# A tuned graph network kernel: POOL runs three waited-for fills behind every fourth row gather

## What is computed

```python
# first part: attention over the edges, and two hops of mean aggregation
msg = alpha[:, :, None] * h[src]
out = jax.ops.segment_sum(msg, dst, num_segments=N)
...
for _ in range(num_hops):
    h = jax.ops.segment_sum(h[src], dst, num_segments=N) / deg
# second part: five layers
for l in range(W1.shape[0]):
    h = _leaky(x @ W1[l] + b1[l]) @ W2[l] + b2[l]
    e = _leaky(edge_attr @ We1[l] + be1[l]) @ We2[l] + be2[l]
    msg = h[src] * e * dot_scale[l]
    agg = jax.ops.segment_sum(msg, dst, num_segments=n)
    out = x + agg * res_w[l]
    ...layer norm...
```

## Time and profile before

| what | us |
|---|---|
| median of 3 runs | 8059.58 |
| lowest and highest run | 8028.11, 8065.32 |
| span of the profiled execution | 8041.5 |
| PE busy | 5609.6 |
| DVE busy | 4833.5 |
| POOL busy | 4208.7 |
| ACT busy | 3995.4 |

### The profile page before, as it was taken

One profiled execution on the slowest core, in us unless ns is written; L12 is line 12 of the kernel. 1 busy time (PEld: TensorE's weight loads), 2 busy tenths in 40 slices (PEclk: granted clock), 3 DMA queues, 4 the chain that ended last, 5 costly groups with the idle time before them and its releaser, 6 DMA issues.

```text
span 8041.5 us, 131647 instructions
## 1 busy us (share of the span) xinstructions
PE 5609.6 (70%) x48820; PEld 4901.3 (61%) x48820; DVE 4833.5 (60%) x12225; ACT 3995.4 (50%) x6886; POOL 4208.7 (52%) x4251
## 2 busy tenths in 40 slices
PE   6787772333333788876788877888867888688886
PEld 5676651222222677776777766777757777577776
DVE  5565565566575566655666665566656666566666
ACT  3454444555564355553555544555535555355554
POOL 4454457666665355554555544555545555455554
PEclk8898775655555788887888887888878888689887
DMA  3333325767675233332233322323323333233322
GB/s 85 83 96 83 84 72 174 233 233 240 233 259 198 52 79 80 83 79 57 80 84 79 82 71 67 79 80 84 81 57 80 84 83 79 56 79 83 83 80 68
DMA packets 509356, 828.41 MB, mean 103 GB/s; under 512 B 112942, under 2 KB 220069, under 8 KB 495662
## 3 DMA queue, kind: packets, MB, share of 16 engines
q1 hardware_dynamic: 373374, 650.98, 24.0%
q0 software_dynamic: 135344, 169.01, 11.5%
HBM read 385.16 MB, written 434.48 MB: 102 GB/s over the span
## 4 chain that ended last, share of the span: by engine, by line
PE 36%; issue 12%; DVE 12%; another core or an unknown queue 7%; POOL 1%; ACT 1%; DMA 0%; DVEq 0%; SPq 0%; POOLq 0%; ACTq 0%
PE psum L1354 30%; DVE arena L1756 5%; PE psum L1368 5%; DVE by_lane L1819 2%; DVE psum L1802 1%; DVE es_w L1756 1%; POOL agg L700 1%; DVE gring L1796 0%; DVE psum L1808 0%; PE psum L1280 0%; PE psum L1311 0%; DVE xin L1756 0%; DVE gring L1756 0%; DMA agg<-rowsg,last_i 0%
## 5 line engine op out<-in xcount | busy, mean ns | idle before, releaser
L693 POOL DMA_INDIRECT gring<-tableh,src_i x2652 | 2600.3, 980 | 2529.9 <-DVE psum L1802 1560.1
L1354 PE MATMUL psum<-penalty,arena 125*128 125x192 bf16 x24736 | 2659.8, 260 | 611.6 <-issue 579.9
L1354 PEld LDWEIGHTS psum<-penalty,arena 125*128 125x128 bf16 x24736 | 2232.7, 103 | 859.3 <-issue 789.4
L693 POOL DMA_INDIRECT gring<-table,src_i x1364 | 1388.7, 1018 | 1031.9 <-issue 402.7
L1756 DVE TENSOR_SCALAR arena<-dst_f,node_id 125x640 bf16<-125x640 f16 x4556 | 1605.1, 401 | 0.1
L1796 DVE TENSOR_REDUCE gring<-psum 128x128 f32<-128x384 f32 x505 | 355.9, 705 | 1996.9 <-remote 1286.4
L967 ACT COPY psum<-diag 128x512 f32<-128x512 f32 x505 | 297.5, 590 | 2355.9 <-DVE psum L1802 2202.9
L1368 PE MATMUL psum<-arena 128*128 128x128 f32 x4040 | 706.3, 311 | 180.1 <-issue 164.8
L1368 PEld LDWEIGHTS psum<-arena 128*128 128x128 f32 x4040 | 601.2, 218 | 243.7 <-issue 241.8
L1486 DVE SCALAR_TENSOR_TENSOR arena<-psum,be_c,arena 128x512 f32<-128x512 f32 x505 | 376.7, 746 | 450.5 <-ACT arena L839 260.1
L839 ACT ACTIVATE arena<-psum,be_leak 128x512 f32<-128x512 f32 x505 | 335.9, 686 | 602.3 <-remote 410.6
(11 more groups left out here) (271 smaller groups left out, 7681.2 us busy)
## 6 DMA issues: line engine op xcount, KB each, us to landing
rows<-arena SPq DMA_DIRECT2D x101, 1296.0 KB
acts<-arena SPq DMA_DIRECT2D x505, 256.0 KB
arena<-acts SPq DMA_DIRECT2D x505, 256.0 KB
rowsg<-run SPq DMA_DIRECT2D x505, 256.0 KB
gring<-tableh,src_i POOLq DMA_INDIRECT x2652
dst_f<-pe_src SPq DMA_DIRECT2D x430, 93.8 KB
rows<-run SPq DMA_DIRECT2D x101, 256.0 KB
gring<-table,src_i POOLq DMA_INDIRECT x1364
```

Of the source, the lines that this page charges most:

```text
L693: pool.indirect_dma_start(ring[:, s, k, :], None, table, bass.IndirectOffsetOnAxis(ap=src_i[:, c * K + k:c * K + k + 1], axis=0))\
L1354: ins = mm(found(n)[:, m, :], hot_at(n // 2, j)[:, at:at + P], parts[:, j, :, :].rearrange("q a f -> q (a f)"), start=(j == 0), stop=(j == ...
```

## The change

POOL gets a helper, `pause`, that fills a scratch tile of 128 x 256 fp32 three times and waits for each fill before it goes on. `gather_chunk`, which all seven passes use, counts its gathers in one counter and calls `pause` before the fifth, the ninth and so on: behind every fourth gather, wherever the chunk borders lie. The gathers of node rows at the ends of the passes are not counted. To have a semaphore for it, `node_id_set` goes; the one instruction that raised it raises `consts_set` instead, whose full count goes up by one.

```diff
+BURST = 4
+REST = 3
...
+        rest = sb("rest", [P, 256])
...
+        rested = sem("rested")
...
             pool.iota(node_id[:, :], [[1, NJ]], base=-MID, channel_multiplier=NJ,
-                      allow_small_or_imprecise_dtypes=True).then_inc(node_id_set, 1)
+                      allow_small_or_imprecise_dtypes=True).then_inc(consts_set, 1)
...
+            issued, rests = [0], [0]
+
+            def pause():
+
+                for _ in range(REST):
+                    pool.memset(rest[:, :], 0.0).then_inc(rested, 1)
+                    rests[0] += 1
+                    pool.wait_ge(rested, rests[0])
+
             def gather_chunk(c, s, table, ring, ready, cols):
                 for k in range(cols):
+                    if issued[0] and issued[0] % BURST == 0:
+                        pause()
+                    issued[0] += 1
                     pool.indirect_dma_start(ring[:, s, k, :], None, table,
...
-            act.wait_ge(node_id_set, 1)
...
-            dve.wait_ge(node_id_set, 1)
...
-            dve.wait_ge(node_id_set, 1)
...
-N_CONSTS = 20
+N_CONSTS = 21
```

More of the change, by code:

```diff
@@ L339, in build @@
         src_in = [sem(f"src_in{b}") for b in range(2)]
-        found_ps, hot_done, parts_ready, node_id_set = (sem(n) for n in (
-            "found_ps", "hot_done", "parts_ready", "node_id_set"))
+        found_ps, hot_done, parts_ready = (sem(n) for n in ("found_ps", "hot_done", "parts_ready"))
         cg_ready, cg_used = sem("cg_ready"), sem("cg_used")
         early_set = sem("early_set")
+        rested = sem("rested")
         be_set = sem("be_set")
```

## The result

| what | before | after |
|---|---|---|
| median, us | 8062.45 (4 runs) | 6963.74 (4 runs) |
| lowest and highest, us | 8028.11, 8078.08 | 6958.54, 6970.45 |
| span of the profiled execution, us | 8041.5 | 6958.6 |

A forecast was written before the change was run, and what follows sets the result against it. The prediction took PE, kept slow in stretches by back-to-back gathers, as the bound: 8041.5 - 252 (layers) - 40 (layer starts) - 50 (hop) + 140 (attention) = 7840, plus 18 from span to median, said as 7860 us; range 7620 to 8260.

The forecast's parts named there:

- the price of a pause: On POOL, behind every fourth gather: three fills and their waits add 1.7 us to the gap, ends 1.4 and 2.0.
- the work of a pause on the slow stretches: On PE in the layers: pauses cut each slow stretch from 7.3 to 4 to 4.5 us.
- One sign of being wrong: In the layers: DVE waiting for gathers would mean POOL is the bound by more than reckoned; no size given.
- What bounds the kernel: Whole kernel: PE, kept slow by back-to-back gathers in 213 stretches, 1561 us; a gap of about 1.9 us ends one.
- The layers: Five layers: a chunk falls from 9.70 to 9.2 us, gaining 252 us, ends 379 us and nothing.
- Layer starts: At each layer's start: a pause breaks the stretch of 21 us, gaining 8 us a layer, 40 us (0 to 75).
- The hop pass: Hop pass: the same stretches, rarer; POOL needs 9.3 us a chunk against 10.8 now; gain 50 us (0 to 120).
- The attention pass: Attention pass: no countable slow stretches, POOL becomes the bound at 1434 us; 140 us longer (78 to 199).
- (a): Whole kernel: runs of four gathers never start a slow stretch, POOL is the bound everywhere; 7626 us, chance 0.15.
- (b): Whole kernel: pauses do not let PE out, stretches last until the run ends; 8680 us, chance 0.13.
- (c): Whole kernel: pauses work, but POOL's waits behind chunk ends and lost ring lead cost the gain; 8020 to 8100, chance 0.10.
- (d): Whole kernel: DVE stretches the pauses to 2.3 us, no gain in layers, attention + 240; about 8250 us, chance 0.10.

The follow-up runs named there:

- e7_before_again: The kernel before, unchanged, run again on a chip where it met hardly any slow stretches: 5724.71 us.
- e8_after_again: The changed kernel, unchanged, run again on a chip where the kernel before took 5724.6 us: 6910.39 us, ratio 1.208 to the kernel before.
- e6_one_fill: Against the changed kernel, one long fill of 1248 one-byte elements replaces the three in each pause: 6920.69 us, 1.209 of the kernel before on that chip.

## Why the prediction was wrong in its size

The steps that failed are two terms of the sum: the price of a pause, put at 1.7 us and measured at 1.15, and the work of a pause on the slow stretches, put at "4 to 4.5 us instead of 7.3" so that PE stays beside POOL as a bound, where no long stretch was left beside the paused gathers and POOL alone is the bound. Of the 896 us by which the measurement lies below the forecast, the layers make 502, the hop pass 172, the attention pass 157, layer starts 28, start-up and the rest 22, and the difference between span and median most of what is left. One sign of being wrong that the prediction named came: DVE waits for gathers in the layers, 395.3 us at L1815.

**What bounds the kernel.** Right where it was read: PE, held back in slow stretches beside long runs of gathers. But "I take it that gathers issued back to back keep PE slow" is too wide. e7_before_again has runs of 530 gathers and no such PE, so the earlier trace rows show a coincidence in time that holds on some chips only. This did not make the number wrong, since the kernel before took 8078.08 us in the one further run that the result has of it; it limits what the change is worth.

**One pause.** Forecast 1.7 us (1.4 to 2.0), measured 1.15 us, below the range's end. The working took three fills of 0.312 us and three waits of 0.24 us. But the 0.24 us of idle time stood before another operation, a select at L665 that waited for a fill, and not between two fills. In the row at 3807.64 three fills and the waits between them last 1.07 us, 0.94 us of it fills at 0.312, which leaves 0.06 us for each of two waits; over the whole trace all 2006 waits between two fills of a pause are 0.057 or 0.058 us. The last wait and the issue of the next gather cost 0.27 us together, in place of the ordinary 0.30, and not on top of it.

**The layers.** Forecast 9.2 us a chunk and 252 us gained; measured 8.25 to 8.32 and 754 us. The two mis-sized terms are the pause (1.31 times 0.55 us too much on POOL's side, 0.72 us a chunk) and the stretches, taken as shortened to 4 to 4.5 us, when none of four gaps was left in the steady part. With both put right POOL's need is 6.67 + 1.31 x 1.15 = 8.18 us a chunk, and that is what is measured within 0.14. The 0.25 us added for two sides waiting for each other was hardly there, at most 0.14: PE, at 744.41 us busy in a stretch of 880 us, has slack:

```profile
3340.00:4220.00 880.00, 744.41 (x7866) 713.09 (x7865) 679.51 (x1607) 535.07 (x719) 679.96 (x949) 0.93 0.35 92
```

The granted clock rose from 0.86 to 0.93, as the prediction's last part asked for. It is 0.91 in the same stretch of e8_after_again, where there are no slow stretches, and 1.00 in e7_before_again. So what it lacks goes with the idle time that the pauses bring: PE and DVE wait for gathers in both.

**Layer starts.** Forecast 40 us (0 to 75), measured 68 us for the tails and starts together: inside the range. The tails were not in the forecast, and they are only in part cured, as shown above: the gathers there are not paused.

**The hop pass.** Forecast 50 us (0 to 120), measured 222 us, 10.81 to 8.58 us a chunk. The same two terms: 5.5 x 1.27 + 1.37 x 1.15 = 8.56 us.

**The attention pass.** Forecast 140 us worse, measured 17 us better. "Has no slow stretches that I could count" failed: the count went by gaps of over 0.45 us between weight loads, and PE has too few of them in this pass for it to show. The waits of the weight load at L1155 (before) and L1169 (after) show it (us, times, longest), of before, of the kernel before where it takes 5725 us, and of after:

```profile
PEld psum L1155 <- issue: 355.8, 101, 19.3
```

```profile
PEld psum L1155 <- issue: 43.8, 101, 5.6
```

```profile
PEld psum L1169 <- issue: 46.6, 101, 8.7
```

So 12.75 us a chunk was a stalled pass, not a clean one; clean it takes 10.36. POOL's need with two pauses, measured at 12.58, came in its place, and that the two are alike is chance. The term was that need, 1434 us, less the 1296 us of before. The form was right, the need was too high: 202 pauses of 1.15 us are 232 us and not 343, and the gathers alone need 101 times 10.36, 1046 us, and not 1091. That makes 1278 us, 18 less than before, where 17 were measured.

**The rivals.** (a), no stretch starts in runs of four, named 7626 us with a chance of 0.15, and what it said of the time came: PE is out of the way and POOL's need is the bound. That no stretch starts is not shown to the letter, see the short gaps above. With 1.15 us in place of 1.7 its own sum would have been: 505 x (9.78 - 8.18) = 808, starts 75, hop 101 x (10.81 - 8.56) = 227, attention the measured 17, together 1127, and with the 18 us over the span 8059.5 - 1127 = some 6930 us, against 6963.74. Its 0.15 rested on "this may be only the phase in which SP's stores fall", though 203 of 213 starts at the fourth to tenth gather was the strongest count of the trace. (b) and (c) did not happen. In (d), "attention + 240" should read 260 by its own numbers (1091 + 202 x 2.3 - 1296). Of (d), a little did: the fills in the layers take 0.368 us on average, not 0.312, while those of the attention pass take 0.317, and DVE's one-hot builds went from 0.401 us over the whole trace to 0.437. (Where there are no stretches, they go from 0.415 us without fills to 0.439 with them.) POOL's fills in the attention pass:

```profile
L708 POOL DMA_INDIRECT gring<-table,src_i x796 | 814.0, 1023 | 239.2 <-issue 184.5 <-POOL rest L699 52.3 <-ACT arena L921 1.4
L699 POOL MEMSET rest<- 128x256 f32 x594 | 188.4, 317 | 22.8
```

That is 0.05 us a fill, some 0.15 us a pause, where (d) had 0.6. The rule of the Trainium skill (SBUF — State Buffer, "Who interferes with whom") that the prediction weighed, by which a fill that meets a one-hot build waits for the whole of it, had been put at 0.2 us a pause: the trace agrees in sign and roughly in size. e6_one_fill shows the same on a longer piece: with one fill of 1.157 us in each pause the builds last 547 ns on average.

```profile
L1769 DVE TENSOR_SCALAR arena<-dst_f,node_id 125x640 bf16<-125x640 f16 x4556 | 2282.0, 547 | 0.1
...
L699 POOL MEMSET rest<- 128x1248 uint8 x1003 | 1160.0, 1157 | 67.4 <-DMA tableh<-arena 67.0
```

**What stays open.** What makes one run of the same program have stretches and another not, and what PE lacks in them, no run shows; the gathers themselves look alike on both. Whether a cheaper setting, above all one fill behind every fourth gather (6114 us where it was measured), would keep the stretches away on a chip that has them was not measured there; if runs of four are what matters and the gap hardly, which the short spells that begin beside them make doubtful, it would gain some 850 us more than the change does. That is an estimate from the clean runs, not a result. No version tried beats the kernel before where it takes 5725 us.

## What to carry to other kernels

Before curing a stall that the profile gives no cause for ("issue" idle on an engine that has its operands), run the unchanged kernel on a second chip and at another time: here the same change is worth 13.4% in one place and costs 20.8% in another. Where one engine's pauses keep another going, price the pause by measuring the gap between the two real neighbours, not by adding up lone waits, and try the shortest pause first, since its whole length is paid as soon as that engine is the bound. A count in the trace that points to one mechanism nineteen times in twenty deserves a larger chance than 0.15. And a count of "stretches" should be repeated with a looser rule before it is said that none begins.

## What the runs showed of the hardware that was not expected

- The same program takes 8028 to 8105 us on some chips and 5711 to 5736 us on others. With it go slow stretches of PE, 213 of them (1561 us of the 2319 us between the two profiled spans) against four (41 us; none with gaps joined as above). No run shows whether it is the chip or the moment. Gathers on POOL last 0.94 to 0.98 us on both.
- On a chip that has them, stretches of four gaps and more start in one in six runs of five gathers and in most runs of nine and more (139 of 166), and practically never in runs of four with a pause of 1.45 us behind them (4 of over 999). A short gap of PE, 4.5 to 6.0 us behind the run's start, is there in 273 of 605 such runs, against 49 of 603 on a chip without stretches.
- A gather costs POOL 0.94 us and 0.30 us of issue, behind another gather. Behind a waited-for fill it starts after 0.27 us. Fills of 0.312 us that are each waited for follow one another after 0.057 us.
- A fill of 128x256 fp32 lasts 0.317 us beside the attention pass's work and 0.368 us in the layers, beside the one-hot builds, and a build on average 0.024 to 0.036 us longer than without fills.
